# Value bias added at the copy of the head outputs, and two banks and another order for the first query/key sums, in an attention-and-dense block

## The reference

```python
x = lax.conv_general_dilated(inputs, conv_w, ...) + conv_b      # 3 taps, 1024 -> 768 = q, k, v of 256
qh = einsum('btd,dhe->bthe', q, wq) + bq                        # 16 heads of 64; blocks of 128 tokens
kh = einsum('btd,dhe->bthe', k, wk) + bk
vh = einsum('btd,dhe->bthe', v, wv) + bv
p = softmax(where(causal, qh * scale @ kh, NEG_INF))
o = einsum('bhqk,bkhe->bqhe', p, vh)
o = einsum('bqhe,hed->bqd', o, wo) + bo
x = x + o @ proj_w + proj_b
# then a dense layer 1024 -> 1024 with four low-rank experts and a softmax gate, added to x
```

## Time and profile before

| | |
|---|---|
| median of 3 runs | 840.63 us (838.38 to 841.25) |
| the profiled execution | 841.22 us, its span 839.4 us |
| PE busy | 799.4 us, 95% of the span |
| DVE, ACT, POOL busy | 462.4, 394.3, 198.3 us |
| mean granted clock of TensorE | 0.988 |
| chain that ended last | PE 77%, DVE 13%, ACT 4% |

### The profile page before, as it was taken

The page is one execution under the profiler, slowest core; times in us unless marked ns, Lnnn a source line. Parts: engine busy times, 40 slices in busy tenths (PEclk is TensorE's granted clock), DMA queues, the critical chain, the costliest instruction groups (busy, mean ns, idle before and its releaser), DMA issues.

```text
span 839.4 us, 14378 instructions
## 1 busy us (share of the span) xinstructions
PE 799.4 (95%) x5280; PEld 711.2 (85%) x5280; DVE 462.4 (55%) x1372; ACT 394.3 (47%) x1069; POOL 198.3 (24%) x178
## 2 busy tenths in 40 slices
PE   3899989999998999999999999999989999999997
PEld 3698877778777888888888888888879999999996
DVE  6888987778877443433333434433574544445441
ACT  5173343344324688686868676766841111111110
POOL 2110012223230235252434343432320100101000
PEclk9999999999999899999999999999999999999999
DMA  8645732534446130121262421203032322313111
GB/s 335 236 132 171 227 127 82 201 121 136 151 138 237 71 114 7 60 76 51 87 239 101 97 101 39 101 2 151 29 99 101 101 54 98 93 60 101 53 49 50
DMA packets 41370, 94.04 MB, mean 112 GB/s; under 512 B 9299, under 2 KB 18387, under 8 KB 40020
## 3 DMA queue, kind: packets, MB, share of 16 engines
q1 hardware_dynamic: 38996, 84.73, 30.3%
q0 software_dynamic: 2304, 8.39, 2.4%
HBM read 66.63 MB, written 26.08 MB: 110 GB/s over the span
## 4 chain that ended last, share of the span: by engine, by line
PE 77%; DVE 13%; ACT 4%; issue 2%; POOL 2%; DMA 0%; DVEq 0%; ACTq 0%
PE net_psum L63 15%; PE net_psum L65 15%; PE net_psum L64 15%; PE net_psum L1119 8%; PE net_psum L1194 5%; PE net_psum L1213 4%; PE net_psum L1205 4%; POOL raw L457 2%; DVE raw L814 2%; PE net_psum L1248 2%; PE net_psum L1249 2%; PE net_psum L1250 2%; PE net_psum L1262 2%; DVE raw L815 1%; PE net_psum L1104 1%
## 5 line engine op out<-in xcount | busy, mean ns | idle before, releaser
L63 PE MATMUL net_psum<-fw_hi,xT_hi 128*128 128x354 f32 (+1 forms) x384 | 125.6, 327 | 0.7 <-DVE xT_lo L946 0.7
L65 PE MATMUL net_psum<-fw_hi,xT_lo 128*128 128x354 f32 (+1 forms) x384 | 124.5, 324 | 0.0
L64 PE MATMUL net_psum<-fw_lo,xT_hi 128*128 128x354 f32 (+1 forms) x384 | 124.4, 324 | 0.0
L474 POOL TENSOR_TENSOR pr<-pr,rrec 128x512 f32<-128x512 f32 x64 | 66.7, 1042 | 227.3 <-DVE rrec L881 227.3
L614 ACT ACTIVATE pr<-pr,negmax 128x128 f32<-128x128 f32 x256 | 99.1, 391 | 11.6 <-DVE negmax L888 11.6
L888 DVE CUSTOM_DVE_ANT_0 pr<-net_psum,mask 128x128 f32<-128x128 f32 x256 | 58.9, 287 | 54.2 <-PE net_psum L1194 54.2
L1119 PE MATMUL net_psum<-ua,wa 128*128 128x256 f32 x384 | 85.3, 384 | 3.3 <-DVE ua L772 3.3
L1119 PEld LDWEIGHTS net_psum<-ua,wa 128*128 128x128 f32 x384 | 73.7, 193 | 13.6 <-issue 3.5
L63 PE MATMUL net_psum<-x_hi,w_hi 128*128 128x512 f32 x192 | 77.6, 404 | 6.5 <-DVE w_lo L821 6.3
L63 PE MATMUL net_psum<-c_hi,wqk_hi 128*128 128x256 f32 x256 | 77.7, 304 | 2.8 <-ACT kf L621 2.8
L64 PE MATMUL net_psum<-x_lo,w_hi 128*128 128x512 f32 x192 | 76.6, 399 | 0.0
(11 more groups left out here) (169 smaller groups left out, 1827.7 us busy)
## 6 DMA issues: line engine op xcount, KB each, us to landing
wa<-in_conv_w SPq DMA_DIRECT2D x24, 512.0 KB, 3.9
raw<-in_conv_w SPq DMA_DIRECT2D x24, 384.0 KB, 3.4
xn<-in_x SPq DMA_DIRECT2D x16, 512.0 KB, 10.1
xr<-in_x SPq DMA_DIRECT2D x8, 1024.0 KB, 5.0
x_scratch<-xr SPq DMA_DIRECT2D x8, 1024.0 KB, 4.0
x1t<-x_scratch SPq DMA_DIRECT2D x16, 512.0 KB, 4.3
out<-y POOLq DMA_DIRECT2D x16, 512.0 KB, 5.0
c_raw<-c_scratch SPq DMA_DIRECT2D x7, 768.0 KB, 4.7
```

The source lines that it names most:

```text
L63: pe.matmul(out, w_hi, x_hi, start=first, stop=False)
L64: pe.matmul(out, w_hi, x_lo, start=False, stop=False)
L65: return pe.matmul(out, w_lo, x_hi, start=False, stop=last)
L474: pool.tensor_tensor(pr[:, jj % 4], pr[:, jj % 4], rrec[:, jj % 4].unsqueeze(2).to_broadcast([P, UN, P]), ALU.mult).then_inc(s["p_ready"], 1)
```

## The change

Three things are changed. `setup_bias`, the sum `ba_c` and their semaphores go; ACT adds `bv` as it copies the head outputs out (`Identity` with a bias in place of `Copy`), DVE's low part does the same in a `scalar_tensor_tensor`, and `a_hi`, `a_lo` take `bo` alone. The two halves of `wo_lo` are made in steps 5 and 6. Sums(1) and sums(3) go to bank 3 (`qk_side`), so that up to step 4 sums(J) waits for `kf` of pair J-2; the first turn waits for `kf` of pair 3 in return. And the first work stands in another order: ACT takes `qf` and `kf` of pair 2 ahead of the exponentials of pair 0, DVE the first maximum ahead of the second piece of the convolution's last block.

```diff
...
@@ -233,6 +233,7 @@
         qkp = psum[:, 0].rearrange("p (k t) -> p k t", k=2)
         scp = psum[:, 1:3]
         ptp = psum[:, 3]
+        qk_side = psum[:, 3].rearrange("p (k t) -> p k t", k=2)
         op = psum[:, 4, 0:GT].rearrange("p (b t) -> p b t", b=GB)
         ap_ = psum[:, 5].rearrange("p (d t) -> p d t", d=WC)
         vy = (psum[:, 6], psum[:, 7])
@@ -288,6 +289,10 @@
 
         def planes_of(t):
             return t.rearrange("p (b k i) -> p b k i", k=4, i=32)
+
+        def qk_acc(J):
+
+            return qk_side if J in (1, 3) else qkp
 
         def is_step(jj):
             return 0 <= jj < NJ
@@ -589,6 +594,21 @@
                     act.activation(c0_hi[:, slot(LAST - 1)], cya[:, 0:GB].rearrange("p b k i -> p (b k i)"), ACT.Copy).then_inc(s["c4_hi_ready"], 1)
                     act.wait_ge(s["early_loaded"], 16 * 4)
 
+            def exponentials(jj):
+                act.wait_ge(s["max_ready"], jj + 1)
+                wait(act, s["rrec_ready"], jj - 1)
+                for un in range(UN):
+                    e = act.activation(pr[:, jj % 4, un], pr[:, jj % 4, un], ACT.Exp, bias=negmax[:, jj % 2, un:un + 1], scale=-1.0,
+                                       accum_out=rsum[:, jj % 2, un:un + 1])
+                e.then_inc(s["exp_ready"], 1)
+
+            def queries_keys(J):
+                i = J % NP
+                act.wait_ge(s["qk_done"], J + 1)
+                wait(act, s["sc_done"], J - 1)
+                act.activation(qf[:, J % 2], qk_acc(J)[:, 0], ACT.Identity, bias=bqk_c[:, 0, i:i + 1])
+                act.activation(kf[:, J % 2], qk_acc(J)[:, 1], ACT.Identity, bias=bqk_c[:, 1, i:i + 1]).then_inc(s["qk_ready"], 1)
+
             def last_c():
 
                 act.wait_ge(s["head_ready"], 1)
@@ -600,7 +620,8 @@
                 if is_step(jj):
                     act.wait_ge(s["o_done"], jj + 1)
                     wait(act, s["a_step"], jj - 1)
-                    act.activation(oT_hi[:, jj % 2], op.rearrange("p b t -> p (b t)"), ACT.Copy).then_inc(s["oT_hi_ready"], 1)
+                    act.activation(oT_hi[:, jj % 2], op.rearrange("p b t -> p (b t)"), ACT.Identity,
+                                   bias=bv_c[:, jj % NP:jj % NP + 1]).then_inc(s["oT_hi_ready"], 1)
                 jj = J - TR
                 if is_step(jj):
                     act.wait_ge(s["pT_done"], jj + 1)
@@ -608,17 +629,9 @@
                     act.activation(pT[:, jj % 2].rearrange("p b t -> p (b t)"), ptp, ACT.Copy).then_inc(s["pT_ready"], 1)
                 jj = J - SC
                 if is_step(jj):
-                    act.wait_ge(s["max_ready"], jj + 1)
-                    wait(act, s["rrec_ready"], jj - 1)
-                    for un in range(UN):
-                        e = act.activation(pr[:, jj % 4, un], pr[:, jj % 4, un], ACT.Exp, bias=negmax[:, jj % 2, un:un + 1], scale=-1.0,
-                                           accum_out=rsum[:, jj % 2, un:un + 1])
-                    e.then_inc(s["exp_ready"], 1)
-                if is_step(J):
-                    act.wait_ge(s["qk_done"], J + 1)
-                    wait(act, s["sc_done"], J - 1)
-                    act.activation(qf[:, J % 2], qkp[:, 0], ACT.Identity, bias=bqk_c[:, 0, i:i + 1])
-                    act.activation(kf[:, J % 2], qkp[:, 1], ACT.Identity, bias=bqk_c[:, 1, i:i + 1]).then_inc(s["qk_ready"], 1)
+                    exponentials(jj)
+                if is_step(J) and J != 2:
+                    queries_keys(J)
                 at = i - (5 if g == 0 else 3)
                 if g + 1 < NG and at in (0, 1):
                     m = slice(3 * at, 3 * at + 3)
...
@@ -726,6 +739,7 @@
             attention_step(0, 0)
             attention_step(0, 1)
             last_c()
+            queries_keys(2)
             attention_step(0, 2)
             for J in range(HEAD, NJ):
                 attention_step(J // NP, J % NP)
@@ -891,12 +905,13 @@
                 jj = J - OT
                 if is_step(jj):
                     dve.wait_ge(s["oT_hi_ready"], jj + 1)
-                    dve.tensor_tensor(oT_lo[:, jj % 2], op.rearrange("p b t -> p (b t)"), oT_hi[:, jj % 2], ALU.subtract).then_inc(s["oT_lo_ready"], 1)
+                    dve.scalar_tensor_tensor(oT_lo[:, jj % 2], op.rearrange("p b t -> p (b t)"), bv_c[:, jj % NP:jj % NP + 1],
+                                             oT_hi[:, jj % 2], ALU.add, ALU.subtract).then_inc(s["oT_lo_ready"], 1)
                 if i == 5 and 0 <= g - 1 < NG:
                     dve.wait_ge(s["a_hi_ready"], g)
                     for d in range(WC):
                         for b in range(GB):
-                            a = dve.scalar_tensor_tensor(by_plane(a_lo[:, d])[:, b], planes_of(ap_[:, d])[:, b], ba_c[:, d:d + 1],
+                            a = dve.scalar_tensor_tensor(by_plane(a_lo[:, d])[:, b], planes_of(ap_[:, d])[:, b], bo_c[:, d:d + 1],
                                                          by_plane(a_hi[:, d])[:, b], ALU.add, ALU.subtract)
                     a.then_inc(s["a_lo_ready"], 1)
                 yu = y_unit(g, i)
@@ -907,12 +922,10 @@
                         dve.wait_ge(s["xb_ready"], GB * e + n // 2 + 1)
                     k, cols = ycols(n)
                     dve.tensor_tensor(xr[:, k, cols], vy[n % 2], xr[:, k, cols], ALU.add).then_inc(s["x1_ready"], 1)
-                if (g, i) == (0, 6):
-                    dve.wait_ge(s["bvo_done"], 1)
-                    dve.tensor_tensor(ba_c[:], ap_[:, 0, 0:WC], bo_c[:], ALU.add).then_inc(s["ba_ready"], 1)
-                    for k in range(2):
-                        dve.wait_ge(s["wo_hi_ready"], k + 1)
-                        dve.tensor_tensor(wo_lo[:, 4 * k:4 * k + 4], wo_raw[:, 4 * k:4 * k + 4], wo_hi[:, 4 * k:4 * k + 4], ALU.subtract).then_inc(s["wo_lo_ready"], 1)
+                if (g, i) in ((0, 5), (0, 6)):
+                    k = i - 5
+                    dve.wait_ge(s["wo_hi_ready"], k + 1)
+                    dve.tensor_tensor(wo_lo[:, 4 * k:4 * k + 4], wo_raw[:, 4 * k:4 * k + 4], wo_hi[:, 4 * k:4 * k + 4], ALU.subtract).then_inc(s["wo_lo_ready"], 1)
                 if (g, i) in ((1, 2), (1, 3)):
                     dve.wait_ge(s["pw_hi_ready"], i - 1)
                     dve.tensor_tensor(pw_lo[:, i - 2], pw_raw[:, i - 2], pw_hi[:, i - 2], ALU.subtract).then_inc(s["pw_lo_ready"], 1)
@@ -1058,18 +1071,20 @@
             sums(LAST, 0, GB).then_inc(s["add_done"], 1)
             dve.wait_ge(s["add_done"], 1)
             ends(LAST, 0, GB).then_inc(s["head_ready"], 1)
-            sums(LAST, GB, 2 * GB).then_inc(s["add_done"], 1)
+            dve.wait_ge(s["mask_ready"], 4)
+            dve.wait_ge(s["early_loaded"], 16 * 4)
+            for J in range(HEAD):
+                attention_step(0, J)
             dve.wait_ge(s["c5_hi_ready"], 1)
             dve.tensor_tensor(c_lo[:, 0, slot(LAST)], cyz[:, 0:GB].rearrange("p b k i -> p (b k i)"), c0_hi[:, slot(LAST)], ALU.subtract).then_inc(s["c5_lo_ready"], 1)
+            sums(LAST, GB, 2 * GB).then_inc(s["add_done"], 1)
             dve.wait_ge(s["add_done"], 2)
             ends(LAST, GB, 2 * GB).then_inc(s["next_ready"], 1)
-            dve.wait_ge(s["mask_ready"], 4)
-            for J in range(HEAD + len(REST)):
+            for J in range(HEAD, HEAD + len(REST)):
                 attention_step(0, J)
-                if J >= HEAD:
-                    sums(LAST, *REST[J - HEAD]).then_inc(s["add_done"], 1)
-                    dve.wait_ge(s["add_done"], 3 + J - HEAD)
-                    e = ends(LAST, *REST[J - HEAD])
+                sums(LAST, *REST[J - HEAD]).then_inc(s["add_done"], 1)
+                dve.wait_ge(s["add_done"], 3 + J - HEAD)
+                e = ends(LAST, *REST[J - HEAD])
             e.then_inc(s["cy_ready"], 1)
             for J in range(HEAD + len(REST), NJ + NP - 1):
                 attention_step(J // NP, J % NP)
@@ -1136,14 +1151,6 @@
                         mm = three_pass(pe, acc[m % 2][:, v, :], w_hi[:, k % WR, v, c % 2], w_lo[:, k % WR, v, c % 2],
                                         x_hi[:, c, v], x_lo[:, c, v], c == 0, c == DC - 1)
                 mm.then_inc(s["unit_done"], 1)
-
-            def setup_bias():
-
-                pe.wait_ge(s["wo_loaded"], 16)
-                for d in range(WC):
-                    for c in range(OC):
-                        mm = pe.matmul(ap_[:, 0, d:d + 1], wo_raw[:, c, d * P:(d + 1) * P], bv_c[:, c:c + 1], start=(c == 0), stop=(c == OC - 1))
-                mm.then_inc(s["bvo_done"], 1)
 
             def values(g, n):
                 if g == 0 and n == 0:
@@ -1208,7 +1215,7 @@
                 jj = J - TR
                 if is_step(jj):
                     pe.wait_ge(s["p_ready"], jj + 1)
-                    wait(pe, s["pT_ready"], jj)
+                    pe.wait_ge(s["qk_ready"], 4) if jj == 0 else pe.wait_ge(s["pT_ready"], jj)
                     for un in range(UN):
```

(11 more changed lines are left out.)

8 lines of the change are left out of this document (4 added, 4 removed).

## The result

The changed kernel takes 832.83 us (median of 5 runs, 831.08 to 834.10), the kernel before 840.99 us (5 runs, 838.38 to 841.30). The ratio is 0.9907, with a 95% interval of 0.9894 to 0.9920. It is faster by 8.16 us; 8.15 had been forecast. The profiled execution of after took 831.08 us, 10.14 less than that of before, and its span is 829.3 us.

A forecast was written before the change was run, and what follows sets the result against it. PE's own work was taken to bound the steady attention. Terms of 3.42 + 3.55 + 1.38 = 8.35 us, less 0.2 at the end, gave 8.15 us and a forecast of 832.5 us, range 830.2 to 836.0.

The forecast's parts named there:

- The first steps: Start of the attention, up to scores(3): new banks and order bring scores(3) from 280.76 to 277.34 us, gain 3.42 us.
- The new wait: PE ahead of the first turn: it waits 1.33 us until ACT's kf of pair 3 empties bank 3.
- The product: Product with bv on PE, ahead of scores(4): its 3.55 us go and nothing on PE replaces it.
- What follows it: Step 6, behind the product with bv: 6.85 us become 5.47 at full clock, gain 1.38 us.
- the gain without both falls: Up to scores(5), against an execution of before without the two clock falls: 5.3 us to gain instead of 8.35.
- ACT and DVE: Head output copies: oT_hi about 0.09 us longer, oT_lo up to 0.48 but taken as nothing; hidden in the steady steps.
- The last steps: From 590 us, where idle cover is thin: the longer ACT copies cost 0.2 us, at most 0.45.
- The wait in the product's place: Rival, steps 4 and 5: PE waits for ACT as long as the product took, 836.0 us; chance 0.08.
- swallowed later: Rival, 590 to 632 us: PE's idle time hangs on transfers and absorbs the gain, 840.5 us; chance 0.05.
- become the bound: Rival, oT_hi in each of the 64 steps: the longer copy makes ACT the bound, slower, 845.9 us; chance 0.03.
- The two rivals on the clock: Clock falls in the new first steps too, 834.2 us, chance 0.15; or holds at the attention's end, 830.8 us, 0.14.

The follow-up runs named there:

- e1: The changed kernel with one bank and the old order put back, the bias kept in the copies: 833.69 us, ratio 0.9917.
- e2: The changed kernel with the bias edits undone, so banks and order are new but the product with bv is kept: 837.94 us, ratio 0.9978.
- e6: The changed kernel plus as many unused one-column matmuls as the product with bv had, at its place: 836.84 us.
- e10: e2 run again unchanged: step 6 took 6.88 us, and scores(5) to the end 542.09 us.
- e11: e6 run again unchanged, on a different chip: 837.58 us.
- e7: The changed kernel plus 30 unused matmuls of 256 columns at the place of the product with bv: 836.98 us.
- e8: The changed kernel with half of each head output copied out a second time on ACT: 835.07 us, ratio 0.9915.
- e12: The changed kernel run again unchanged: 833.87 us.
- e4: The changed kernel with all first sums in one bank, the new order kept: 832.79 us, ratio 0.9915.
- e3: The changed kernel with ACT's and DVE's old order in the first steps, two banks kept: 832.98 us, ratio 0.9905.
- e5: The changed kernel with ACT's copies of pair 3 put ahead of the exponentials of pair 1: 832.36 us, ratio 0.9898.

## Why the prediction was right, and which step was not

**The total.** 832.83 us measured, 832.5 forecast. In the two profiled executions it was made from, the parts agree too: 3.36 for 3.42, then 3.47 (8.27 - 4.80) for 3.55, then 1.51 for 1.38, 8.34 in all for 8.35. That is agreement with one execution of before, and less than it seems.

**The first steps, the step that was mis-sized.** The order of events came as it was laid out: scores(0) to scores(3) at 2.94, 5.50, 9.14 and 14.61 us, where the prediction's times give 3.00, 5.59, 9.20 and 14.55. The new wait is 1.40 us for 1.33, the one of scores(1) 0.23 for 0.45. But what they were compared with was not the program's. Of the 3.42 us, 1.67 were lost clock, which the term booked as won; the fall measured 1.53 (17.97 - 16.44). Of 14 profiled executions here, three ran the first steps with one bank and the old order: before, where the clock fell, before again and e1, where it did not. It fell there in none of the eleven others. The change itself is worth 1.78 to 1.85 us in these steps. That the new order also makes a fall there rarer is not shown by one in three against none in eleven.

**The product.** 3.47 us, in e2, e6, e10, e11 and both executions of before alike. The step holds.

**What follows it.** The term of 1.38 measured 1.5 us (6.85 - 5.34, or 6.88 - 5.34), since step 6 at full clock takes 5.33 and not 5.47. It is a fall of the clock and not the work: e6 and e11 show both cases of one program. With one-column matmuls at that place the clock fell behind them in 5 of 6 executions (before twice, e2, e10, e11; not e6). So the product made that fall likely, not certain, and the change removes its occasion: without those matmuls there was none in the seven executions that had nothing at that place. With the wide ones of e7 there was none either, in one execution, which is too few to say that the single columns matter. The Trainium skill, "TensorE: Matmul & The Clock Gate", Part 1, says that the check runs freely; that a fall may for this reason come in one execution and not in the next was the prediction's inference. E6 and e11 agree with it, 5.33 and 6.87 us. The prediction put the gain without both falls at 5.3 us. The rows give that: e6, which differs from after by such a stretch alone and had no fall, comes to scores(5) 28.25 - 24.75 = 3.50 us later, and 3.50 + 1.78 = 5.28.

**ACT and DVE.** `oT_hi` took 475 ns, inside the 0.46 to 0.48. `oT_lo` took 59 ns more where I took nothing, inside its bounds. Both are hidden in the steady steps, as the 294 us windows and e8 show. The last steps were to cost 0.2 us. PE's last two waits for `oT_lo` there are 0.53 and 0.93 us in after and e12, 0.47 and 0.86 to 0.87 in both executions of before, in e2 and in e10: 0.12 to 0.13 us more. In the executions in which the clock stayed at 1.00 there, the stretch from scores(5) to the end is 542.23 to 542.28 with the bias in the copies (e1, e4, e11) and 542.09 without (e10): 0.14 to 0.19 us, from one execution on the one side. Where the clock falls there, in the ten others, it is 543.39 to 544.22, and such a difference is lost.

**The rivals.** The wait in the product's place did not come: ACT was busy 10.94 of 11.30 us but never late. Nothing was swallowed later. ACT did not become the bound, not even in e8. The two rivals on the clock name what did vary: its fall in the last steps came in both executions of after and stayed away in four of the others, so that it came and went by execution, as the prediction had put it.

**Why the total still came out.** Both kernels' runs lie some 3 us apart, and in the profiles the stretch ahead of the attention alone moves the first sums from 261.15 to 263.56 us in two executions of after. The window of 16 to 34 us of after:

```profile
16.00:34.00 18.00, 11.90 (x72) 10.50 (x73) 14.09 (x29) 8.35 (x9) 2.14 (x3) 1.00 0.88 334
```

The same window of after, run again (e12):

```profile
16.00:34.00 18.00, 12.74 (x62) 10.94 (x63) 13.54 (x29) 8.35 (x9) 2.14 (x3) 0.81 0.78 305
```

The clock is 1.00 in the one and 0.81 in the other, and PE gets 72 records done against 62.

All 14 executions fall into three groups: the first sums start at 261.15 us where the mean clock of the first 34 us is 1.00 (one execution of after), at 262.79 to 263.04 where it is 0.95 (nine), and at 263.56 to 264.43 where it is 0.90 (four).

The two pairs of profiled executions differ by 841.22 - 831.08 = 10.14 and 839.91 - 833.87 = 6.04 us; the medians' 8.16 lies in the middle. In the second pair, 0.69 of the change's 6.86 us go to the later first sums of after and 0.17 to its end.

Each timed run comes with the mean granted clock of the execution, and that tells more. The five runs of after have 0.991 to 0.995, median 0.993; the twenty runs of before that were timed beside e1 to e8 have 0.987 to 0.991, median 0.989. Where the clock is 0.991 in both, before takes 839.99 to 840.21 us (four runs) and after 833.87 to 834.10 (three, e12 among them). So about 6.0 of the 8.16 us are there at an equal clock, and about 2 come with the higher clock of after. This is rough, since the mean does not say where the clock fell: the eight runs of before at 0.989 reach from 839.79 to 841.21.

One fall takes about 0.002 from the mean clock: an estimate, 10.40 x (1 - 0.84) = 1.66 us in a span of some 835. By it the medians lie two falls apart. One of them is the fall behind the product, 1.5 us, which goes with the change. Where the other one was cannot be told, since the timed runs show no place. It seems to go with the product too: on one chip, the ten runs of e2, which keeps it, have 0.985 to 0.993, mean 0.989, as before has there, and the twelve of e1, e3 and e4, which do not, have 0.991 to 0.995, mean 0.994. That would also be why e1 gained 6.93 us where the product and the step behind it make 3.47 + 1.54 = 5.01. How it comes about is open. The spread within e2 also shows that the falls differ between executions of one kernel on one chip.

The change's own terms come to 6.86 us, less 0.13 at the end. The other 1.4 of the 8.16 us came with the higher clock of the runs of after, for which the sum had no term. The 1.67 us booked for a fall in the first steps happened to be about as large. That part of the agreement was luck.

## What to carry to other kernels

When a stretch of the profile shows a granted clock under 1, profile the same program a second time before the lost time is entered as a gain: here 1.5 of 3.4 us in one term were gone in the next execution. Read the mean clock of the timed runs beside their times: here it showed that about 2 of 8.16 us came with a higher clock. Count from an event inside the program (here the first sums), since that showed parts of 0.7 to 3.5 us to within 0.1, where the totals of one kernel spread by 3 us. A wait that is moved by an order should be followed one step further: e5 removed 1.40 us and got 1.00, since a later copy on ACT, which was busy without a break, then set the pace.

## What was not expected of the hardware

The same instructions behind the same 3.5 us of one-column matmuls ran at a clock of 1.00 in one execution (5.33 us) and at a mean of 0.75 in another (6.87 us), on another chip; on one chip, the ten runs of e2 differ in mean clock from 0.985 to 0.993. A fall cost about 1.5 us at each of the three places where it could be told apart: 1.53 in the first steps (17.97 - 16.44), 1.54 behind the one-column matmuls, and 1.30 and 1.53 in the last steps (e2 against e10 and e6 against e11, 543.39 - 542.09 and 543.76 - 542.23).
